# Four-layer transformer on one core: who scales the centred keys of the first attention

## The reference, cut to what matters

```python
kv = kv * cos + _rotate_half(kv) * sin
...
def _ln(x, g, b, eps=1e-05):
    m = jnp.mean(x, axis=-1, keepdims=True)
    v = jnp.var(x, axis=-1, keepdims=True)
    return (x - m) / jnp.sqrt(v + eps) * g + b
...
lkv = jnp.concatenate([prev, lkv_w], axis=2)
lkv = _ln(lkv, ln_local_g, ln_local_b)
lsim = jnp.einsum('bwid,bwjd->bwij', lq, lkv)
...
v = jnp.concatenate([jnp.broadcast_to(gkv[:, None], ...), lkv], axis=-2)
```

## Time and profile before

| | us |
|---|---|
| median of 3 runs | 1810.45 (1801.05 to 1811.97) |
| the profiled execution, its own time | 1807.5 |
| its span | 1805.7 |

### The profile page before, as it was taken

How to read it: one execution, slowest core, us unless ns; L and a number is a source line. 1 busy time by engine, 2 the same in 40 slices (tenths; PEclk the granted TensorE clock), 3 DMA queues, 4 the chain that set the end, 5 groups by cost and what they waited for, 6 DMA issues and landing times. The chain is left out here.

```text
span 1805.7 us, 31707 instructions
## 1 busy us (share of the span) xinstructions
PE 1392.6 (77%) x8970; PEld 1106.4 (61%) x8970; DVE 1086.0 (60%) x2581; ACT 940.3 (52%) x2739; POOL 813.9 (45%) x824
## 2 busy tenths in 40 slices
PE   2368687868787887598898898895799889889552
PEld 0245464545554565488898898895366666666452
DVE  4575666657584743554744746543378887888512
ACT  1256454546454554466666666664456555555110
POOL 2563535355463711355566465565434444342103
PEclk7588786888787888699999999998789999989576
DMA  6200000000000000502002000002411111120064
GB/s 212 95 1 3 0 8 2 7 3 6 8 0 8 1 8 7 206 10 108 8 11 108 7 12 9 11 12 69 135 27 30 25 33 34 30 32 10 12 175 119
DMA packets 127187, 72.32 MB, mean 40 GB/s; under 512 B 78296, under 2 KB 118488, under 8 KB 126680
## 3 DMA queue, kind: packets, MB, share of 16 engines
q1 hardware_dynamic: 116664, 60.95, 11.9%
q0 software_dynamic: 3200, 6.56, 1.4%
q10 hardware_dynamic: 7200, 3.41, 0.6%
HBM read 53.26 MB, written 17.12 MB: 39 GB/s over the span
## 5 line engine op out<-in xcount | busy, mean ns | idle before, releaser
L1401 POOL TENSOR_TENSOR hl<-hid,hh 128x256 fp32r<-128x256 f32 x396 | 292.6, 741 | 223.5 <-ACT hh L1378 219.8
L1444 DVE SCALAR_TENSOR_TENSOR hid<-GU,gub,sg 128x256 f32<-128x256 f32 x396 | 190.4, 482 | 195.0 <-ACT sg L1372 115.9
L1272 PE MATMUL GU<-xh,wh 128*128 128x256 f32 x792 | 234.0, 295 | 39.9 <-DVE wl L1420 30.8
L1372 ACT ACTIVATE sg<-GU,gub 128x256 f32<-128x256 f32 x396 | 187.9, 475 | 125.0 <-PE GU L1274 123.7
L1273 PE MATMUL GU<-xl,wh 128*128 128x256 f32 x792 | 226.1, 285 | 0.0
L1274 PE MATMUL GU<-xh,wl 128*128 128x256 f32 x792 | 226.0, 285 | 0.0
L1808 ACT ACTIVATE prob<-S,negmax 128x256 f32<-128x256 f32 x256 | 118.9, 469 | 162.6 <-DVE negmax L2193 162.6
L613 ACT ACTIVATE prob<-prob,rZ 128x272 f32<-128x272 f32 (+1 forms) x256 | 98.9, 460 | 167.5 <-DVE rZ L978 163.8
L1272 PEld LDWEIGHTS GU<-xh,wh 128*128 128x128 f32 x792 | 152.9, 193 | 49.6 <-issue 27.7
L1378 ACT CAST hh<-hid 128x256 fp32r<-128x256 f32 x396 | 158.1, 399 | 27.3 <-DVE hid L1444 25.8
L1273 PEld LDWEIGHTS GU<-xl,wh 128*128 128x128 f32 x792 | 153.2, 193 | 0.0
(11 more groups left out here) (289 smaller groups left out, 3328.6 us busy)
## 6 DMA issues: line engine op xcount, KB each, us to landing
raw<-in_expert_w SPq DMA_DIRECT2D x4, 2688.0 KB, 12.2
modb<-mod_d SPq DMA_DIRECT2D x2, 2688.0 KB, 15.0
list<-zero SPq DMA_DIRECT2D x5, 1024.0 KB, 9.6
raw<-in_expert_w SPq DMA_DIRECT2D x4, 1152.0 KB, 6.4
wa<-in_w SPq DMA_DIRECT2D x16, 256.0 KB, 3.7
wb<-in_w SPq DMA_DIRECT2D x16, 256.0 KB, 4.2
kpad<-rel_d SPq DMA_DIRECT2D x1, 3072.0 KB, 13.3
qkv_d<-qkvT SPq DMA_DIRECT2D x24, 128.0 KB, 4.6
```

The lines of the kernel that those rows point to most:

```text
L1272: pe.matmul(out, lhs[0], rhs[0], start=start, stop=False, skip_group_check=True)
L1372: act.activation(sg[:, c % BUFS], GU[c % BUFS][:, 0:TT], ACT.Silu, bias=gub[:, GATE, e * CH0 + c:e * CH0 + c + 1]).then_inc(silu, 1)
L1401: pool.tensor_tensor(hl[:, b], hid[:, b], hh[:, b].bitcast(F32), ALU.subtract).then_inc(hid_lo, 1)
L1444: dve.scalar_tensor_tensor(out=hid[:, c % BUFS], in0=GU[c % BUFS][:, TT:2 * TT], scalar=gub[:, UP, e * CH0 + c:e * CH0 + c + 1], in1=sg[:, ...
```

## The change

For each tile ACT now multiplies `kvc` by `krs`, head by head: 16 ACTIVATE of 128x64 with the head's column of `krs` as the scale, 32 for each batch. This stands in ACT's order at the end of the heads' work of hp 3 (tile 0) and of hp 4 (tile 1, ahead of the segment exponential L660). POOL's two operations of L1094 go; its gain for a tile waits for ACT's scaling of that tile (`kv_scaled`), and its wait for earlier readers of V moves to ACT. The counts of `kv_norm` go from 6 to 4 for each batch.

```diff
--- before.py
+++ after.py
@@ -290,7 +290,7 @@
         ln_rstd = sem("ln_rstd")
         kv_rot = sem("kv_rot")
         kv_a = sem("kv_a"); kv_r = sem("kv_r"); kv_mean = sem("kv_mean"); kv_c = sem("kv_c")
-        kv_sq = sem("kv_sq"); kv_ss = sem("kv_ss"); kv_norm = sem("kv_norm")
+        kv_sq = sem("kv_sq"); kv_ss = sem("kv_ss"); kv_norm = sem("kv_norm"); kv_scaled = sem("kv_scaled")
         lg_mul = sem("lg_mul"); lg_red = sem("lg_red"); seg_step = sem("seg_step"); seg_exp = sem("seg_exp")
         wk_done = sem("wk_done")
         g_step = sem("g_step"); g_sq = sem("g_sq"); g_norm = sem("g_norm")
@@ -439,7 +439,7 @@
 
             def kT_mm(slot, b, bp, c):
                 if c == 0:
-                    pe.wait_ge(kv_norm, 6 * (b + 1))
+                    pe.wait_ge(kv_norm, 4 * (b + 1))
                 bank, a = use(f"kT{c}", slot)
                 for u in range(2):
                     for k in range(TILES):
@@ -613,6 +613,15 @@
                         i = act.activation(part, part, ACT.Copy, scale=rZ[:, pb, t, e:e + 1])
                 i.then_inc(p_norm, 1)
 
+            def scale_values(b, bp, t):
+                act.wait_ge(kv_rstd, b + 1)
+                if not known_zero(b - 1):
+                    act.wait_ge(o_mm, HP * (b - 1))
+                for h in range(H0):
+                    head = slice(h * DH0, (h + 1) * DH0)
+                    i = act.activation(V[:, bp, t, head], kvc[:, t, head], ACT.Copy, scale=krs[:, t, h:h + 1])
+                i.then_inc(kv_scaled, 1)
+
             def slot_program(slot, bp):
                 heads, early, late, _ = parts(slot)
                 np_ = 1 - bp
@@ -655,6 +664,8 @@
                         t = hp - 2
                         act.wait_ge(kv_c, 2 * b + t + 1)
                         act.activation(kvs[:, t, :], kvc[:, t, :], ACT.Square).then_inc(kv_sq, 1)
+                    if early and hp in (3, 4):
+                        scale_values(b, np_, hp - 3)
                     if early and hp == 4:
                         bank0.wait_emptied(act, "lgT", slot)
                         act.activation(seg[:, 1, :], seg[:, 0, :], ACT.Exp).then_inc(seg_exp, 1)
@@ -772,7 +783,7 @@
             def kv_center(b, t):
                 dve.wait_ge(kv_mean, 2 * b + t + 1)
                 if not known_zero(b):
-                    dve.wait_ge(kv_norm, 6 * b)
+                    dve.wait_ge(kv_scaled, 2 * b)
                 dve.scalar_tensor_tensor(out=heads_of(kvc[:, t, :]), in0=mean[:, t, :, None].broadcast_to([P, H0, DH0]),
                                          scalar=-1.0 / DH0, in1=heads_of(kvr[:, t, :]), op0=ALU.mult,
                                          op1=ALU.add).then_inc(kv_c, 1)
@@ -825,7 +836,7 @@
                 for t in range(TILES):
                     dve.tensor_tensor(heads_of(wk[:, t, :]), heads_of(kvr[:, t, :]),
                                       pk[:, t, :, None].broadcast_to([P, H0, DH0]), ALU.mult).then_inc(wk_done, 1)
-                dve.wait_ge(kv_norm, 4)
+                dve.wait_ge(kv_norm, 2)
                 for t in range(TILES):
                     dve.tensor_tensor(heads_of(V[:, bp, t, :]), heads_of(V[:, bp, t, :]),
                                       lng[:, 1, None, :].broadcast_to([P, H0, DH0]), ALU.add).then_inc(kv_norm, 1)
@@ -1087,19 +1098,13 @@
                 pool.tensor_tensor(krs[:].rearrange("p t h -> p (t h)"), krs[:].rearrange("p t h -> p (t h)"),
                                    half[:],
                                    ALU.pow).then_inc(kv_rstd, 1)
-                pool.wait_ge(kv_rstd, b + 1)
-                if not known_zero(b - 1):
-                    pool.wait_ge(o_mm, HP * (b - 1))
                 for t in range(TILES):
-                    pool.tensor_tensor(heads_of(V[:, bp, t, :]), heads_of(kvc[:, t, :]),
-                                       krs[:, t, :, None].broadcast_to([P, H0, DH0]), ALU.mult).then_inc(kv_norm, 1)
-                for t in range(TILES):
-                    pool.wait_ge(kv_norm, 6 * b + 1 + t)
+                    pool.wait_ge(kv_scaled, 2 * b + 1 + t)
                     pool.tensor_tensor(heads_of(V[:, bp, t, :]), heads_of(V[:, bp, t, :]), per_head(lng[:, 0, :]),
                                        ALU.mult).then_inc(kv_norm, 1)
                 if not known_zero(b):
                     for t in range(TILES):
-                        pool.wait_ge(kv_norm, 6 * b + 3 + t)
+                        pool.wait_ge(kv_norm, 4 * b + 1 + t)
                         pool.tensor_tensor(heads_of(V[:, bp, t, :]), heads_of(V[:, bp, t, :]), per_head(lng[:, 1, :]),
                                            ALU.add).then_inc(kv_norm, 1)
```

## The result

The changed kernel takes 1864.83 us (median of 4 runs, 1854.61 to 1871.05); the kernel before, over the same comparison, 1805.75. The ratio is 1.0324, with a 95% interval of 1.0255 to 1.0394: 46 to 71 us slower. The forecast was 1853 us, +43 to +46. The profiled execution of the changed kernel (1871.05 us) is the slowest of its four, 6 us above their median, so differences between the two profiles come out somewhat large.

A forecast was written before the change was run, and what follows sets the result against it. It took POOL's chain behind `krs` to bound each slot. Seven slots at 5.76 us (40.3) plus slot -1 (5.3) gave 45.6 us on 1807.5: 1853 us, range (8 in 10) 1832 to 1871.

The forecast's parts named there:

- The bound: First attention's slots: no engine is full; POOL's chain behind `krs` sets the slot, DVE waiting for its layer-norm power.
- The price of a scaling: ACT's head-wise 128x64 multiply by `krs`: 0.235 us each, 3.76 us for 16, bounds 0.17 and 0.33.
- the dear: Rival, chance 0.10: each ACT scaling pays its whole duration, 0.33 us, giving 1878 us.
- the cheap rival: Rival, chance 0.06: ACT's small scalings follow each other at 0.06 us, giving about 1808 us, not slower.
- The step between the tiles: ACT's whole step 4, standing between the scalings of tile 0 and tile 1, delays POOL by 4.29 us.
- the clock's rival: Rival, chance 0.14: PE's idle time is split, its clock stays at 2.4 GHz, saving 2.3 us in 7 slots: 1837.
- The sum to the biases: Slots 0 to 6, `krs` ready to POOL's biases: 14.46 us, less 8.70 before, so 5.76 later; 40.3 in seven slots.
- POOL behind the gains: POOL's biases, layer-norm power and `weigh` in each slot stay unchanged in length, only later.
- Slot -1: Slot without heads: both tiles in one go, then table load, exponential and DVE's weighing; 14.08 less 8.74, 5.3 us longer.
- nothing but a later start: The later layers only start later; no extra time was forecast there.
- The period of a slot: Sign to look for in the profile: heads' periods of about 88 us in place of 82 to 84.
- this mechanism: Shared-port rival, chance 0.04: DVE, stretched beside POOL's wide operations, gains up to 3.69 us at L747 in 6 slots: 1831.

The follow-up runs named there:

- the first experiment: The changed kernel with both tiles scaled in one block at the end of step 3, instead of one at step 3 and one at step 4: ratio 1.0253.

## Why the prediction was right, point by point

**The bound.** It read the slot as POOL's chain behind `krs`, and that a longer chain is paid in full is shown from both sides: with 5.6 us more on POOL alone in each slot the kernel took 2.4% longer, and doubled scalings gave their 7.65 us a slot. That DVE waits at its end for the layer-norm power alone was true too, but the wait is not worth its length: with the power early, 2.5 of 5.6 us were left, because DVE's next operations then ran beside POOL's wide ones. For the change this made no difference, since all of POOL's work shifted together.

**The price of a scaling.** 0.235 us was taken, 0.239 measured, within the bounds; the guess from the 128x144 form less its columns was good to 2%. Neither the dear nor the cheap rival came.

**The step between the tiles.** 4.29 us was taken, 4.55 measured. PE, idle for 8.65 us ahead of it, transposed at 1.2 GHz (the first three in 0.90 us, 0.55 in the kernel before at this step), and ACT's copy of the result waited for it, as one sentence against the clock's rival said it might:

```profile
400.42 0.90 PE L485 MATMUL PT<-const,prob 128*128 128x128 f32 x3 [8.65 <-ACT prob L613]
```

The sum to the biases was 14.46 and is 14.72. The 8.70 that was taken from it counts from the start of POOL's scaling; from the point where `krs` is ready, where the sum begins, it is 8.85. By that the forecast for a slot was 0.15 us too high, 1 us in seven slots, which hid a part of the miss.

**POOL behind the gains.** "Unchanged" was wrong by a little: the biases took 5.02 to 5.04 us in place of 4.63 to 4.83, and DVE now works beside them. That this is the cause is not shown: with both tiles at step 3 DVE worked beside them too, and they took 4.66. With this, `krs` to weigh is 43.8 us longer over seven slots against 40.3.

**Slot -1.** 5.3 was forecast, with the late table load; 4.9 came, and 0.3 lies ahead of it, before the change could act.

**What was missed.** The prediction let everything from weigh to the next `krs`, and the later layers, see "nothing but a later start". That left out 10.5 and 4.0 us of the profiled execution. The first goes with the granted clock in that stretch: the same code takes 68 us in one slot and 72 in another of one execution, and in the profile with PE kept busy at steps 6 and 7 the stretches were 22 us shorter. The period of a slot, for which the prediction named about 88 us as a sign, was 92.2 in slots 1 to 4 and 88.4 in slot 5. The clock's rival had the sign wrong: it let a shorter idle time at step 6 pay back 16 us. PE's idle time at step 6 did shrink, in slot 3 from 8.98 to 2.21 us; but a new one of 8.65 us stands at step 4, the clock was 0.50 from there to 416.4, and behind the 2.21 us PE was at the 1.2 GHz level once more (its transposes at 422.09 take 0.90 us again).

**What stays open.** Which shift of a slot leads to the long stretch and which to the short one was not found; no experiment placed it at will. The length of the idle time alone does not decide it: behind 2.21 us at step 6 PE was at the 1.2 GHz level in slot 3 of the changed kernel, behind 2.22 us in slot 5 at 2.4 GHz. That slower products of PE at step 6 lie on the path is seen in the trace; that the clock causes all of the 10.5 us, and does not merely go with them, is argued and not shown. The 4.0 us behind slot 6 may be nothing: what comes there took between 1165 and 1184 us in the profiled executions of this study. By the interval (46 to 71 us) the forecast lies at or just under its lower end. The two terms that the change itself makes, slot -1 and `krs` to weigh, came to 49 us against the 46 forecast; the mechanism was right, and the total, 1853 us, was 12 us under the measured median.

## What to carry to other kernels

Moving an operation to an engine with idle time helps only if that idle time lies where the operation's input is ready: ACT was idle for 3.4 us ahead of `krs`, then had step 4 to do, and the 10.51 us of idle time ahead of its step 6 came too late for POOL. In the kernel before:

```profile
385.27 1.54 ACT L613 ACTIVATE prob<-prob,rZ 128x272 f32<-128x272 f32 x4 [10.51 <-DVE rZ L978]
```

Look at what stands between two parts of the moved work in the new engine's order, since the next engine waits for that too; placing the same scalings behind the step instead of around it took two thirds of the loss away, and splitting the tiles between both engines turned it into a gain of 0.6%. And the length of a wait is not what its removal brings: here the work behind it moved beside POOL's wide operations, where it took about five times as long (2.34 and 1.90 us for 0.43 and 0.42).

## What the runs showed of the hardware

- ACTIVATEs of 128x64 with a scale from memory, 0.333 us long, start 0.239 us apart (16 in 3.83 us, 32 in 7.64).
- After waits of 8.65 and 12.48 us PE's work still ran at the 1.2 GHz level at step 5, though it had been busy nearly all the time since the wait (in the changed kernel from 400.42 to 406.84 with one pause of 0.95 us; L454: 2.07 us for four products; 1.13 at 2.4 GHz). In the first experiment this put PE on the path; in the changed kernel it did not.
- Three of DVE's operations in fp32, on 128x128 and 128x256, are stretched beside POOL's wide ones, until one of these ends: L747's pair 3.7 us (0.6 in slot -1, where POOL was idle), L750 and L752 2.34 and 1.90 for 0.43 and 0.42. Where POOL's own operations grew, it was by less: its pair of biases in slot 3 from 4.64 to 5.03. This is how the Trainium skill, page "SBUF — State Buffer", section on the two separate sides, describes it: an exclusive lock for a whole instruction, and the other waits. The prediction gave this mechanism 0.04 as a rival and looked in it for time that the change would free; what it does to a DVE that comes earlier it did not price.
